# A latent-expert stage: norms split and moved, the second weights awaited at their first use

## The chip, the core and the metric

The kernel runs on one core of a Trainium2 chip. The metric is the device time of one execution in microseconds. The core has five engines that run their own instruction streams and meet through semaphores: TensorE (PE, matrix products and transposes), VectorE (DVE), ScalarE (ACT), GpSimd (POOL) and SyncE (SP, which issues the transfers here). Each stream is in order: an instruction that waits holds up all behind it on that engine.

## The reference, cut to what matters

The program is four blocks of attention and feed-forward. The change lies in the third feed-forward, a mixture of eight experts and a shared one, over 2048 tokens of width 256:

```
h = x @ down_w + down_b                      # latent, width 128
logits = x @ router_w + router_b - COST_LAMBDA * cost
probs = softmax(logits);  topv, topi = top_k(probs, 2);  gate = softmax(topv)
for k in range(2):
    mask = one_hot(topi[..., k], E)
    for e, (w1, b1, w2, b2) in enumerate(expert_params):
        hm = h * mask[..., e:e + 1]
        acc = acc + (gelu(gelu(hm) @ w1 + b1) @ w2 + b2)
    out = out + acc * gate[..., k:k + 1]
out = out + 0.1 * (gelu(gelu(h) @ shared_w1 + shared_b1) @ shared_w2 + shared_b2)
out = out @ up_w + up_b + gelu(x) @ core_w + core_b
```

Here x is the layer-normalized stream, and the result is added to the stream. An expert that a token did not choose still adds the constant gelu(b1) @ w2 + b2, which the kernel computes once.

## The kernel before, in words

The stage is the function latent_experts. Tokens are taken in four blocks b of 512. The hidden layers of all experts, laid side by side, are 21 tiles n of 128 rows, so that the main loop runs over G = 21 b + n, 84 steps in all, on every engine.

**One step of the main loop.** TensorE multiplies the block's latent by the first weights of the tile (hidden, lines 2330 to 2332). Each fp32 factor is held as a rounded upper part and a rest, so one product is three matmuls of 512 columns. ScalarE applies the gelu in place in PSUM (line 2258). VectorE multiplies by the gate row of the expert into the tile prod (line 2168), a ring of six slots. ScalarE rounds it (upper, line 2232, for the step two back), GpSimd subtracts to get the rest (h_low, line 2045), and TensorE multiplies both by the second weights (project, lines 2345 to 2347) four steps behind hidden. So hidden(G) needs prod of step G-3, and project(G-4) needs h_low of step G-4.

**What is woven into the first 13 steps.** The norms of blocks 1 to 3 are one buffer deep. For each block VectorE takes statistics (line 91) and aggregates them (line 95), GpSimd raises them to the power -1/2 (lines 114 and 116), VectorE applies the norm into ln.xn (line 102), TensorE transposes it (turn, line 2290) and multiplies by the router (route, line 2299, 16 matmuls of 8 columns), ScalarE copies the transposes out of PSUM (keep_turned, line 2195), and VectorE takes the logits (keep_logits, line 2071). After the logits of block 3 come the second softmax and the choice of experts for blocks 1 to 3 (shift, choose, place, weigh).

**Ahead of the loop.** The same is done for block 0, and with it: the first weights w1 are split (ScalarE line 2244, VectorE line 2148), the second weights w2 are split (ScalarE line 2249, VectorE line 2153), twenty small matmuls on w2 make the constant of the unchosen experts (line 2375; ScalarE keeps it at line 2251), the gates are transposed (line 2320) and kept (line 2220), written to memory and read back broadcast into the tile gb (line 2028), and the latent is split (ScalarE lines 2209 and 2213, VectorE line 2125). The raw w1 lies in the second half of gb and the raw w2 in the ring prod, so prod can't be written before w2 is split and the small matmuls are done. In the trace both weight tiles are called f_w_high and f_w_low, and f_gb and f_prod stand for their raw copies.

The order is written by hand: no planner sets it. The whole of the front part and the step numbers at which pieces are woven in stand in the four engine programs below.

Of the kernel before, what the change touches and what calls it, by code (L numbers as in the profile page):

```python
# [87 lines left out]
def layer_norm_stats(dve, n, b, source):  # L88

    for t in range(n.tiles):  # L90
        dve.bn_stats(n.stats[:, t, :], source(t)).then_inc(n.stats_done, 1)  # L91
    dve.wait_ge(n.stats_done, n.tiles * (b + 1))
    dve.memset(n.held[:, 0:1], 0.0)
    for t in range(n.tiles):
        dve.bn_aggr(n.mv[:, t, :], n.stats[:, t, :]).then_inc(n.meanvar_done, 1)
# [1836 lines left out]
def latent_experts(nc, tag, X, cst, PS, gate_rows, t):  # L1932
# [9 lines left out]
    with ExitStack() as ctx:  # L1942
# [61 lines left out]
        with nc.Block() as block:  # L2004
# [26 lines left out]
            @block.gpsimd  # L2031
            def _(pool):
                pool.memset(ln.eps[:, :], EPS).then_inc(preset, 1)
                pool.memset(neg_half[:, :], -0.5).then_inc(preset, 1)
                pool.memset(zb[:, :, :], 0.0).then_inc(preset, 1)
                pool.memset(gates[:, :, :], 0.0).then_inc(preset, 1)
                pool.wait_ge(preset, 4)
                pool.memset(gates[:, :, NE:NX], SHARED_GATE).then_inc(preset, 1)
                for b in range(NB - 1):
                    layer_norm_pool(pool, ln, b, neg_half)  # L2040
                for G in range(FULL):
                    pool.wait_ge(h_high_done, G + 1)
                    if G >= 6:
                        pool.wait_ge(y_done, G - 5)
                    pool.tensor_tensor(h_low[:, G % 6, :], prod[:, G % 6, :], h_high[:, G % 6, :].bitcast(F32),  # L2045
                                       ALU.subtract).then_inc(h_low_done, 1)
                    if G == 2:
                        layer_norm_pool(pool, ln, 3, neg_half)

            @block.vector  # L2050
            def _(dve):
# [7 lines left out]
                def source(b):  # L2059
                    return lambda k: X[:, TB * b + k, :]  # L2060

                def norm(b):

                    layer_norm_stats(dve, ln, b, source(b))
                    if b:
                        dve.wait_ge(transposed, KC * b)
                    layer_norm_apply(dve, ln, b, source(b))
# [66 lines left out]
                def add_bias(b, k):  # L2134
                    dve.tensor_tensor(X[:, TB * b + k, :], X[:, TB * b + k, :], outb[:, 0, :], ALU.add).then_inc(biased, 1)

                norm(0)
                dve.wait_ge(loaded_front, 64)
                then(dve.tensor_tensor(rb[:, :], rb[:, :], cst[:, C_COST:C_COST + NE], ALU.subtract))
                dve.wait_ge(gb1_done, 1)  # L2140
                for e in range(NE):
                    f = first[e]
                    z = dve.tensor_copy(zb[:, f:f + EXPERT_TILES[e], e], gb1[:, f:f + EXPERT_TILES[e]])
                z.then_inc(zb_done, 1)
                keep_logits(0)
                shift(0, 0, TB)
                dve.wait_ge(w1_high_done, 1)
                dve.tensor_tensor(w1_low[:, :, :], w1_in, w1_high[:, :, :].bitcast(F32), ALU.subtract).then_inc(w1_low_done, 1)
                choose(0, 0, TB)
                place(0, 0, TB)  # L2150
                weigh(0, 0, TB)
                dve.wait_ge(w2_high_done, 1)
                dve.tensor_tensor(w2_low[:, :, :], w2_in, w2_high[:, :, :].bitcast(F32), ALU.subtract).then_inc(w2_low_done, 1)
                latent_low(0)
                dve.wait_ge(loaded_back, 80)
                then(dve.tensor_tensor(outb[:, 0, :], outb[:, 0, :], outb[:, 1, :], ALU.add))
                norm(1)
                norm(2)
                dve.wait_ge(d_done, 1)
                for G in range(FULL):  # L2160
                    b, n = G // NHT, G % NHT
                    e = expert_of[n]
                    dve.wait_ge(act_done, G + 1)
                    if n == first[e]:
                        dve.wait_ge(gb_loaded[b % 2][e], 16 * (b // 2 + 1))
                    if G >= 6:
                        dve.wait_ge(h_low_done, G - 5)
                    dve.tensor_tensor(prod[:, G % 6, :], PS[:, HB[G % 3], :], gb[:, b % 2, e, :], ALU.mult).then_inc(prod_done, 1)  # L2168
                    if b == 0 and n in (4, 6, 9):
                        keep_logits((4, 6, 9).index(n) + 1)  # L2170
                    if b == 0 and n == 4:
                        norm(3)
                    if b == 0 and n == 9:
                        shift(1, TB, NT)
                    if b == 0 and n == 10:
                        choose(1, TB, NT)
                    if b == 0 and n == 11:
                        place(1, TB, NT)
                    if b == 0 and n == 12:
                        weigh(1, TB, NT)  # L2180
                    if n == 14 and b + 1 < NB:
                        latent_low(b + 1)
                    if n in (15, 16, 17, 18):
                        add_bias(b, n - 15)
                    if b and n in (9, 10):
                        add_outputs(b - 1, n - 9)
# [4 lines left out]
            def _(act):  # L2191
# [53 lines left out]
                exponent(0, 0, TB)  # L2245
                second(0, 0, TB)
                latent(0)
                act.wait_ge(loaded_w2, 16)
                act.activation(w2_high[:, :, :], w2_in, ACT.Copy).then_inc(w2_high_done, 1)
                act.wait_ge(d_done, 1)  # L2250
                act.activation(dsum[:, :], PS[0:NE, 3, 0:LAT], ACT.Copy).then_inc(d_kept, 1)
                keep_gates(0)
                act.wait_ge(c_done, 1)
                act.activation(consts[:, :], PS[0:NX, 3, LAT:2 * LAT], ACT.Copy).then_inc(c_kept, 1)
                for G in range(FULL):
                    b, n = G // NHT, G % NHT
                    act.wait_ge(h_done, G + 1)
                    act.activation(PS[:, HB[G % 3], :], PS[:, HB[G % 3], :], ACT.Gelu, bias=b1[:, n:n + 1]).then_inc(act_done, 1)  # L2258
                    if b == 0 and n in (2, 4, 7):
                        keep_turned((2, 4, 7).index(n) + 1)  # L2260
                    if G >= 2:
                        upper(G - 2)
                    if b == 0 and n == 10:
                        exponent(1, TB, NT)
                    if b == 0 and n == 11:
                        second(1, TB, NT)
                    if n == 4 and b:
                        keep_outputs(b - 1)
                    if n == 13 and b + 1 < NB:
                        latent(b + 1)  # L2270
                    if n in (17, 18):
                        core_input(b, n - 17)
                    if n == 15 and b + 1 < NB:
                        keep_gates(b + 1)
# [5 lines left out]
            def _(pe):  # L2280
# [53 lines left out]
                def project(G):  # L2334
                    b, n = G // NHT, G % NHT
                    out = PS[:, 2 + b % 2, :]
                    if n == 0:
                        pe.wait_ge(gT_kept, b + 1)
                        if b == 0:
                            pe.wait_ge(c_kept, 1)  # L2340
                        if b >= 2:
                            pe.wait_ge(y_kept, b - 1)
                        pe.matmul(out, consts[:, :], gT[0:NX, :], start=True, stop=False).then_inc(const_done, 1)
                    pe.wait_ge(h_low_done, G + 1)
                    pe.matmul(out, w2_high[:, n, :], h_high[:, G % 6, :], start=False, stop=False)
                    pe.matmul(out, w2_low[:, n, :], h_high[:, G % 6, :], start=False, stop=False)
                    pe.matmul(out, w2_high[:, n, :], h_low[:, G % 6, :], start=False, stop=(n == NHT - 1)).then_inc(y_done, 1)
# [33 lines left out]
                pe.matmul(PS[0:NX, 3, LAT:2 * LAT], cst[0:NX, C_BSUM:C_BSUM + NX], b2[:, :], start=False,  # L2381
                          stop=True).then_inc(c_done, 1)
                pe.wait_ge(w1_low_done, 1)
                pe.wait_ge(w2_low_done, 1)
                for G in range(FULL + LAG):
                    b, n = G // NHT, G % NHT
                    if G < FULL:
                        hidden(G)
                    if G >= LAG:
                        project(G - LAG)  # L2390
                    if G < FULL:
                        if b == 0 and n in (2, 4, 7):
                            turn((2, 4, 7).index(n) + 1)
                        if b == 0 and n in (3, 5, 8):
                            route((3, 5, 8).index(n) + 1)
                        if n == 12 and b + 1 < NB:
                            latent(b + 1)
                        if n == 14 and b + 1 < NB:
                            turn_gates(b + 1)
                        if b and n in (6, 8):  # L2400
                            outputs(b - 1, (n - 6) // 2)
# [603 lines left out]
```

## Time and profile before

| | us |
|---|---|
| median of 3 runs | 1897.74 |
| lowest and highest | 1887.23, 1900.02 |
| the profiled execution | 1893.01 |
| its span, first to last instruction | 1891.2 |

The page of the profile gives, over the whole span, TensorE 86% busy, VectorE 62%, ScalarE 46%, GpSimd 25%, at a mean granted TensorE clock of 0.939 of 2.4 GHz. The latent-expert stage is the stretch from about 1217 to 1434 us of it. Times in the rows are microseconds from the start of the span. A busy time of a matmul overlaps that of its neighbour, so the pace of TensorE is read from the distance between starts.

### The profile page before, as it was taken

The page shows a single profiled execution, that of the slowest core. Times are in us where ns is not written, and L with a number is a line of the kernel's source. Part 1 is how long each engine was busy: PE and PEld are TensorE (multiplying, and loading weights), DVE is VectorE, ACT ScalarE, POOL GpSimd, SP SyncE. Part 2 cuts the span into 40 slices and gives each one's busy share as a digit, 9 for nine tenths or more (in the row PEclk, how much of TensorE's full clock was granted, in tenths as well). Part 3 has the DMA queues.
Part 4 walks back from the last instruction along what each step waited for, and adds up shares of the span by engine and source line. Part 5 has one row for each costly group of instructions (what it writes and reads, how often), then busy time and mean ns, then how long its engine had stood idle before and what let it go on. Part 6 is the DMA issues. An engine that isn't in the chain of part 4 may idle for free. (4 is left out here: it accounts for less than half of the span.)

```text
span 1891.2 us, 28840 instructions
## 1 busy us (share of the span) xinstructions
PE 1619.8 (86%) x10648; PEld 945.2 (50%) x10654; DVE 1172.8 (62%) x2595; ACT 869.0 (46%) x1360; POOL 477.5 (25%) x594
## 2 busy tenths in 40 slices
PE   4899999899999999801599999779999999998776
PEld 2344444488756566501346655456775344443533
DVE  2687887333246666479767776355553787774475
ACT  1255666432225554541125555447672466665322
POOL 4222210033213330030323230026673422210100
PEclk9899999999999999955799999979999999999698
DMA  7342240100055424010345523111114345320322
GB/s 245 98 123 80 78 123 1 67 0 0 32 156 157 116 77 123 1 51 0 96 119 140 156 79 80 73 55 52 51 51 134 93 111 156 88 69 2 119 90 90
DMA packets 68688, 162.29 MB, mean 86 GB/s; under 512 B 10013, under 2 KB 15526, under 8 KB 67562
## 3 DMA queue, kind: packets, MB, share of 16 engines
q1 hardware_dynamic: 68554, 160.52, 29.9%
q8 instruction: 82, 1.34, 0.3%
q14 instruction: 52, 0.43, 0.1%
HBM read 111.06 MB, written 53.09 MB: 87 GB/s over the span
## 5 line engine op out<-in xcount | busy, mean ns | idle before, releaser
L1078 DVE TENSOR_REDUCE a_mx<-PS 128x1 f32<-128x512 f32 (+3 forms) x768 | 394.8, 552 | 191.6 <-PE PS L1320 129.1
L1261 ACT ACTIVATE a_pT<-PS 128x1024 f32<-128x1024 f32 (+3 forms) x384 | 310.4, 812 | 213.6 <-PE PS L1344 151.7
L1315 PE MATMUL PS<-a_k,a_q 64*128 64x512 f32 (+3 forms) x768 | 231.5, 413 | 10.5 <-DVE a_mx L1078 6.3
L405 DVE CUSTOM_DVE_ANT_0 PS<-PS,a_dist 128x448 f32<-128x448 f32 x256 | 156.2, 643 | 51.6 <-PE PS L650 49.3
L1335 PE MATMUL PS<-a_q,a_k 64*128 64x512 f32 (+3 forms) x768 | 172.0, 434 | 6.8 <-issue 5.0
L1358 PE MATMUL PS<-a_pT,a_va 128*32 128x512 f32 (+3 forms) x1536 | 163.6, 498 | 5.6 <-ACT a_raw L1219 5.4
L122 PE MATMUL PS<-cst 128*128 128x512 f32 x248 | 128.4, 646 | 44.2 <-PEq L66 35.3
L555 ACT ACTIVATE a_pT<-PS 128x448 f32<-128x448 f32 (+1 forms) x256 | 124.6, 540 | 86.3 <-PE PS L673 86.0
L1315 PEld LDWEIGHTS PS<-a_k,a_q 64*128 64x128 f32 x768 | 109.9, 185 | 79.2 <-DVE a_mx L1078 60.7
L1335 PEld LDWEIGHTS PS<-a_q,a_k 64*128 64x128 f32 x768 | 74.6, 183 | 143.4 <-issue 67.0
L2045 POOL TENSOR_TENSOR f_h_low<-f_prod,f_h_high 128x512 fp32r<-128x512 f32 x84 | 110.3, 1321 | 61.0 <-ACT f_h_high L2232 56.3
L2168 DVE TENSOR_TENSOR f_prod<-PS,f_gb 128x512 f32<-128x512 f32 x84 | 57.5, 688 | 70.2 <-ACT PS L2258 68.1
L650 PE MATMUL PS<-a_k,a_q 64*128 64x448 f32 x256 | 86.3, 465 | 12.7 <-DVE a_mx L405 5.5
L1196 ACT ACTIVATE a_q<-PS 16x1024 fp32r<-16x1024 f32 x48 | 48.8, 1016 | 91.8 <-PE PS L1366 91.4
L122 PEld LDWEIGHTS PS<-cst 128*128 128x128 f32 x248 | 45.0, 200 | 89.9 <-issue 81.8
L1318 PE MATMUL PS<-a_half_masks 64*128 64x128 bf16 x512 | 86.1, 227 | 0.0
L2258 ACT ACTIVATE PS<-PS,f_b 128x512 f32<-128x512 f32 x84 | 55.5, 660 | 50.6 <-PE PS L2332 50.3
L1320 PE MATMUL PS<-a_half_masks 64*128 64x64 bf16 x512 | 72.3, 189 | 0.0
L1029 POOL TENSOR_TENSOR a_mxh<-a_mx,a_m 128x16 fp32r<-128x16 f32 x48 | 10.9, 227 | 240.6 <-DVE a_mx L1078 240.6
L686 PE MATMUL PS<-a_pT,a_va 128*32 128x512 f32 x512 | 68.2, 604 | 1.5 <-ACT a_raw L563 1.1
L1506 POOL TENSOR_TENSOR f_h_low<-f_hid,f_h_high 128x512 fp32r<-128x512 f32 x32 | 41.1, 1289 | 101.9 <-ACT f_h_high L1571 101.9
L1083 DVE TENSOR_SCALAR a_q<-PS 16x1024 fp32r<-16x1024 f32 x48 | 59.0, 1230 | 6.0 <-PE PS L1366 4.6
(355 smaller groups left out, 3419.6 us busy)
## 6 DMA issues: line engine op xcount, KB each, us to landing
spread_scratch<-a_high SPq DMA_DIRECT2D x96, 256.0 KB, 3.5
a_q<-spread_scratch SPq DMA_DIRECT2D x96, 256.0 KB, 5.5
a_k<-spread_scratch SPq DMA_DIRECT2D x96, 256.0 KB, 6.5
f_gb<-gate_rows SPq DMA_DIRECT2D x68, 256.0 KB, 5.4
spread_scratch<-a_low SPq DMA_DIRECT2D x48, 256.0 KB, 4.5
a_q<-window_scratch SPq DMA_DIRECT2D x32, 256.0 KB, 5.4
a_k<-window_scratch SPq DMA_DIRECT2D x32, 256.0 KB, 6.3
window_scratch<-a_high SPq DMA_DIRECT2D x24, 256.0 KB, 4.7
```

Of the source, the lines that this page charges most:

```text
L122: pe.matmul(PS[:, bank, :], cst[:, C_ID:C_ID + P], cst[:, 0:512], start=True, stop=True)
L405: dve.tensor_tensor_reduce(PS[:, 4 + a, 0:KW], PS[:, 4 + a, 0:KW], dt_[:, off:off + KW], 1.0, 3e38, ALU.add, ALU.min, mx[:, gg % 2, qt, 2 ...
L555: act.activation(pT[rows, buffer_of(kt), 2 * half + a, GLOB:S], PS[rows, 2 * half + a, GLOB:S], ACT.Exp, scale=-float(slopes[2 * pair + a] ...
L650: pe.matmul(PS[:, 4 + a, 0:KW], q[rows, b % 2, pair, qt * P:(qt + 1) * P], k[rows, b % 2, pair, GLOB:S], start=True, stop=True).then_inc(s ...
L1078: dve.tensor_reduce(mx[:, gg % 2, qt, 2 * half + a:2 * half + a + 1], PS[:, 4 + a, 0:kw], AX.X, ALU.max).then_inc(max_done, 1)
L1261: act.activation(pT[:, N // 2 % 2, N % 2, :, q0:S], PS[:, 2 * (N % 2):2 * (N % 2) + 2, q0:S], ACT.Exp, scale=SCALE).then_inc(exp_done, 1)
L1315: mm = pe.matmul(ps[:, 0:kw], q[rows, b % 2, pair, qt * P:(qt + 1) * P], k[rows, b % 2, pair, 0:kw], start=True, stop=not causal)
L1318: pe.matmul(ps[:, kw - P:kw], half_masks[rows, 0, 0, :], half_masks[rows, 1, 0, :], start=False, stop=False)
L1320: mm = pe.matmul(ps[:, kw - 64:kw], half_masks[rows, 0, 1, :], half_masks[rows, 1, 1, 64:P], start=False, stop=True)
L1335: mm = pe.matmul(PS[:, 2 * half + a, q0:S], k[rows, b % 2, pair, kt * P:(kt + 1) * P], q[rows, b % 2, pair, q0:S], start=True, stop=not ca ...
L1358: mm = pe.matmul(PS[BLK * i:BLK * i + BLK, 6, q0:S], va[:, b % 2, kt, GH * g + i, :], pT[:, J % 2, i // 2, i % 2, q0:S], start=(kt == 0), ...
L2045: pool.tensor_tensor(h_low[:, G % 6, :], prod[:, G % 6, :], h_high[:, G % 6, :].bitcast(F32), ALU.subtract).then_inc(h_low_done, 1)
```

## The change

All of it is in latent_experts. The norm of a block is split into statistics and application, which can now stand apart. VectorE does both for block 1 before it reads the first logits, the statistics of block 2 before it splits w2, and applies block 2 after step 1 of the loop; block 3 has its statistics after step 3 and its application after step 5 (before: blocks 1 and 2 whole ahead of the loop, block 3 after step 4). The split of w1 on VectorE goes behind the softmax and the gates of block 0. ScalarE splits w2 behind the two copies that it stood ahead of. TensorE waits for the split w2 in project(0) and no longer ahead of the loop. The turns go from steps 2, 4, 7 to 0, 3, 6, the routes from 3, 5, 8 to 1, 4, 7. The sum of two bias rows moves from ahead of the loop to step 6.

```
@@ GpSimd
-                    if G == 2:
+                    if G == 1:
                         layer_norm_pool(pool, ln, 3, neg_half)
@@ VectorE
-                norm(0)
+                layer_norm_stats(dve, ln, 0, source(0))
+                normal(0)
...
+                layer_norm_stats(dve, ln, 1, source(1))
+                normal(1)
                 keep_logits(0)
                 shift(0, 0, TB)
-                dve.wait_ge(w1_high_done, 1)
-                dve.tensor_tensor(w1_low[:, :, :], w1_in, w1_high[:, :, :].bitcast(F32), ALU.subtract).then_inc(w1_low_done, 1)
                 choose(0, 0, TB)
                 place(0, 0, TB)
                 weigh(0, 0, TB)
+                dve.wait_ge(w1_high_done, 1)
+                dve.tensor_tensor(w1_low[:, :, :], w1_in, w1_high[:, :, :].bitcast(F32), ALU.subtract).then_inc(w1_low_done, 1)
+                latent_low(0)
+                layer_norm_stats(dve, ln, 2, source(2))
                 dve.wait_ge(w2_high_done, 1)
                 dve.tensor_tensor(w2_low[:, :, :], w2_in, w2_high[:, :, :].bitcast(F32), ALU.subtract).then_inc(w2_low_done, 1)
-                latent_low(0)
-                dve.wait_ge(loaded_back, 80)
-                then(dve.tensor_tensor(outb[:, 0, :], outb[:, 0, :], outb[:, 1, :], ALU.add))
-                norm(1)
-                norm(2)
                 dve.wait_ge(d_done, 1)
+                dve.wait_ge(w2_low_done, 1)
                 for G in range(FULL):
...
-                    if b == 0 and n in (4, 6, 9):
-                        keep_logits((4, 6, 9).index(n) + 1)
-                    if b == 0 and n == 4:
-                        norm(3)
+                    if b == 0 and n in (2, 5, 8):
+                        keep_logits((2, 5, 8).index(n) + 1)
+                    if b == 0 and n == 1:
+                        normal(2)
+                    if b == 0 and n == 3:
+                        layer_norm_stats(dve, ln, 3, source(3))
+                    if b == 0 and n == 5:
+                        normal(3)
+                    if b == 0 and n == 6:
+                        dve.wait_ge(loaded_back, 80)
+                        then(dve.tensor_tensor(outb[:, 0, :], outb[:, 0, :], outb[:, 1, :], ALU.add))
@@ ScalarE
                 latent(0)
-                act.wait_ge(loaded_w2, 16)
-                act.activation(w2_high[:, :, :], w2_in, ACT.Copy).then_inc(w2_high_done, 1)
                 act.wait_ge(d_done, 1)
                 act.activation(dsum[:, :], PS[0:NE, 3, 0:LAT], ACT.Copy).then_inc(d_kept, 1)
                 keep_gates(0)
+                act.wait_ge(loaded_w2, 16)
+                act.activation(w2_high[:, :, :], w2_in, ACT.Copy).then_inc(w2_high_done, 1)
...
-                    if b == 0 and n in (2, 4, 7):
-                        keep_turned((2, 4, 7).index(n) + 1)
+                    if b == 0 and n in (0, 3, 6):
+                        keep_turned((0, 3, 6).index(n) + 1)
@@ TensorE
                         if b == 0:
                             pe.wait_ge(c_kept, 1)
+                            pe.wait_ge(w2_low_done, 1)
...
                 pe.wait_ge(w1_low_done, 1)
-                pe.wait_ge(w2_low_done, 1)
...
-                        if b == 0 and n in (2, 4, 7):
-                            turn((2, 4, 7).index(n) + 1)
-                        if b == 0 and n in (3, 5, 8):
-                            route((3, 5, 8).index(n) + 1)
+                        if b == 0 and n in (0, 3, 6):
+                            turn((0, 3, 6).index(n) + 1)
+                        if b == 0 and n in (1, 4, 7):
+                            route((1, 4, 7).index(n) + 1)
```

VectorE between the gates of block 0 and the first products of the loop. Before (f_w_low<-f_prod is the split of w2, the L91 to L102 rows are norms):

```order
L2118 TENSOR_TENSOR f_gates<-f_hots 128x4x8
L2153 TENSOR_TENSOR f_w_low<-f_prod,f_w_high 128x2688
L2125 TENSOR_TENSOR f_lat_low<-f_lat,f_lat_high 128x512
L2156 TENSOR_TENSOR f_outb<-f_outb 128x256
L91 BN_STATS f_ln_stats<-X 128x6 x4
```

and now (f_w_low<-f_gb is the split of w1):

```order
L2117 TENSOR_TENSOR f_gates<-f_hots 128x4x8
L2153 TENSOR_TENSOR f_w_low<-f_gb,f_w_high 128x2688
L2124 TENSOR_TENSOR f_lat_low<-f_lat,f_lat_high 128x512
L91 BN_STATS f_ln_stats<-X 128x6 x4
L93 MEMSET f_ln_held 128x1
L95 BN_AGGR f_ln_meanvar<-f_ln_stats 128x2 x4
L2157 TENSOR_TENSOR f_w_low<-f_prod,f_w_high 128x2688
L2168 TENSOR_TENSOR f_prod<-PS,f_gb 128x512 x2
L102 TENSOR_SCALAR f_ln_xn<-X,f_ln_meanvar,f_ln_rstd 128x256 x4
```

The two whole norms that stood between the split latent and the first product are gone from there; one half norm and the split of w2 stand there instead, and the application of block 2 stands behind two products.

TensorE at the start of the loop. Before:

```order
L2381 MATMUL PS<-f_b,cst 9x128
L2330 MATMUL PS<-f_lat_high,f_w_high 128x512
L2331 MATMUL PS<-f_lat_low,f_w_high 128x512
L2332 MATMUL PS<-f_lat_high,f_w_low 128x512
L2330 MATMUL PS<-f_lat_high,f_w_high 128x512
L2331 MATMUL PS<-f_lat_low,f_w_high 128x512
L2332 MATMUL PS<-f_lat_high,f_w_low 128x512
```

and now:

```order
L2389 MATMUL PS<-f_b,cst 9x128
L2337 MATMUL PS<-f_lat_high,f_w_high 128x512
L2338 MATMUL PS<-f_lat_low,f_w_high 128x512
L2339 MATMUL PS<-f_lat_high,f_w_low 128x512
L2297 MATMUL PS<-cst,f_ln_xn 128x128 x8
L2337 MATMUL PS<-f_lat_high,f_w_high 128x512
L2338 MATMUL PS<-f_lat_low,f_w_high 128x512
L2339 MATMUL PS<-f_lat_high,f_w_low 128x512
L2306 MATMUL PS<-f_router,f_xnT 128x8 x8
```

The turn of block 1 now stands after one step instead of three, and its route after two instead of four.

## Rows read from the trace of the kernel before

**Rows 1.** Stretches of the stage: start:end, length, busy time by engine (instructions), PEclk, DMA.

```profile
1240.00:1255.00 15.00, 7.17 (x22) 4.75 (x22) 10.78 (x31) 5.23 (x10) 2.41 (x4) 0.51 0.50 160
...
1255.00:1272.00 17.00, 17.00 (x65) 13.33 (x66) 5.81 (x16) 6.36 (x11) 6.25 (x6) 0.63 0.00 0
...
1285.00:1300.00 15.00, 11.12 (x36) 7.74 (x35) 11.78 (x43) 11.19 (x18) 7.04 (x6) 0.77 0.02 4
...
1320.00:1420.00 100.00, 99.44 (x409) 73.27 (x407) 51.90 (x75) 72.23 (x124) 71.45 (x54) 1.00 0.15 48
```

**Rows 2.** The same view in slices of 2 us; PEclk is the granted clock.

```profile
1240.00:1242.00 2.00, 0.67 (x4) 0.37 (x4) 0.84 (x1) 1.76 (x3) 0.00 (x0) 0.58 0.00 0
...
1266.00:1268.00 2.00, 2.00 (x8) 1.70 (x8) 0.00 (x0) 1.66 (x4) 0.14 (x1) 0.60 0.00 0
```

**Rows 3.** TensorE in order of time: start, duration, work [idle before <-releaser].

```profile
1232.96 4.53 PE L2375 MATMUL PS<-f_prod,f_zb 128*8 128x128 f32 x40
...
1238.27 0.63 PE L2320 MATMUL PS<-cst,f_gates 128*128 128x128 f32 x4 [0.78 <-DVE f_gates L2118]
...
1244.86 0.76 PE L2330 MATMUL PS<-f_lat_high,f_w_high 128*128 128x512 f32 x1 [2.51 <-DVE f_lat_low L2125]
1245.42 0.63 PE L2331 MATMUL PS<-f_lat_low,f_w_high 128*128 128x512 f32 x1
1245.85 0.63 PE L2332 MATMUL PS<-f_lat_high,f_w_low 128*128 128x512 f32 x1
...
1255.00 0.80 PE L2330 MATMUL PS<-f_lat_high,f_w_high 128*128 128x512 f32 x1 [3.21 <-DVE f_prod L2168]
...
1261.27 2.07 PE L2343 MATMUL PS<-f_gT,f_consts 9*128 9x512 f32 x2
...
1270.38 0.39 PE L2331 MATMUL PS<-f_lat_low,f_w_high 128*128 128x512 f32 x1
1270.61 0.39 PE L2332 MATMUL PS<-f_lat_high,f_w_low 128*128 128x512 f32 x1
...
1273.80 1.10 PE L2290 MATMUL PS<-cst,f_ln_xn 128*128 128x128 f32 x8 [0.70 <-DVE f_ln_xn L102]
...
1276.13 1.85 PE L2299 MATMUL PS<-f_router,f_xnT 128*128 128x8 f32 x16
1277.83 0.47 PE L2330 MATMUL PS<-f_lat_high,f_w_high 128*128 128x512 f32 x1
```

**Rows 4.** VectorE in order of time, same columns.

```profile
1234.67 0.18 DVE L2085 TENSOR_REDUCE f_den<-f_probs 128x4 f32<-128x32 f32 x1
...
1237.96 0.19 DVE L2118 TENSOR_TENSOR f_gates<-f_hots 128x32 f32<-128x32 f32 x1
1241.16 2.96 DVE L2153 TENSOR_TENSOR f_w_low<-f_prod,f_w_high 128x2688 fp32r<-128x2688 f32 x1 [3.01 <-ACT f_w_high L2249]
...
1245.09 1.40 DVE L91 BATCH_NORM_STATS2 f_ln_stats<-X 128x6 f32<-128x256 f32 x4
...
1248.38 1.38 DVE L102 TENSOR_SCALAR f_ln_xn<-X,f_ln_meanvar,f_ln_rstd 128x256 f32<-128x256 f32 x4 [1.47 <-POOL f_ln_rstd L116]
...
1254.26 1.88 DVE L2168 TENSOR_TENSOR f_prod<-PS,f_gb 128x512 f32<-128x512 f32 x3
...
1270.49 3.26 DVE L102 TENSOR_SCALAR f_ln_xn<-X,f_ln_meanvar,f_ln_rstd 128x256 f32<-128x256 f32 x4 [5.90 <-POOL f_ln_rstd L116]
```

**Rows 5.** ScalarE in order of time, same columns.

```profile
1232.85 0.23 ACT L2199 ACTIVATE f_probs<-f_expo 128x32 f32<-128x32 f32 x1
...
1238.70 2.43 ACT L2249 ACTIVATE f_w_high<-f_prod 128x2688 fp32r<-128x2688 f32 x1
...
1251.82 0.60 ACT L2195 ACTIVATE f_xnT<-PS 128x512 f32<-128x512 f32 x1 [0.26 <-PE PS L2290]
```

**Rows 6.** GpSimd in order of time, same columns.

```profile
1270.35 1.29 POOL L2045 TENSOR_TENSOR f_h_low<-f_prod,f_h_high 128x512 fp32r<-128x512 f32 x1
```

**Rows 7.** Transfers into the tile gb, 1240 to 1300 us: issue to landing.

```profile
DMA to landing us min/median/max: 3.1/4.4/7.0
```

More of the change, by code:

```diff
@@ L2060, in source, with normal @@
                     return lambda k: X[:, TB * b + k, :]
-                def norm(b):
-                    layer_norm_stats(dve, ln, b, source(b))
+                def normal(b):
                     if b:
```

## The prediction, made before the changed kernel was run

> **What bounds the kernel now.** I read the stretches of the stage first. From 1320 to 1420 us TensorE is busy 99.44 of 100 us at the full clock [rows 1]: the main loop is bound by TensorE, and nothing in it is touched beyond step 12. The time to be had lies at its start. From 1240 to 1255 TensorE is busy 7.17 of 15 us at a granted 0.51, and from 1255 to 1272 it is busy throughout, but at a mean of 0.63 [rows 1]. The 2 us slices place the two ends of this: the clock fell from 2.4 to 1.2 GHz within 1240 to 1242 (0.58) and rose again within 1266 to 1268 (0.60) [rows 2]. What TensorE did before it fell: its small matmuls on w2 ended at 1237.49 (1232.96 + 4.53), the gate transposes at 1238.90, and then it mostly waited; the first step of the loop starts at 1244.86, released by the rest of the latent on VectorE [rows 3]. It waits once more, 3.21 us to 1255.00, for the first products of VectorE [rows 3], which start only at 1254.26 [rows 4], behind two whole norms.
>
> What clock it has is seen in the pace of equal matmuls: 0.43 us from start to start at 1245 (1245.42 to 1245.85), 0.23 at 1270 (1270.38 to 1270.61) [rows 3].
>
> As the finish line I take the start of hidden(9), now at 1277.83 [rows 3]. By then both orders have issued the same work on TensorE: 9 steps of hidden, 5 of project, three turns and three routes. Behind it the order is as before, apart from the last logits, one step earlier, and TensorE sets the pace to the end of the stage, so what is won there should reach the end.
>
> **Ahead of the loop.** The exponentials of block 0 were ready at 1233.08 (1232.85 + 0.23) [rows 5], but their sum started at 1234.67, since the split of w1 stood between [rows 4]. With that split behind the gates, the sum starts 1.6 us earlier and the gates are done at 1236.55 in place of 1238.15 (1237.96 + 0.19) [rows 4]. Then comes the split of w1, as large as that of w2, 2.96 us [rows 4], to 1239.5, and the rest of the latent. Before, hidden(0) started 0.74 us after the split in front of it ended (1241.16 + 2.96 = 1244.12, to 1244.86) [rows 3, 4]; so now at 1240.3. That is **4.6 us earlier**. The 3.01 us that VectorE waited for ScalarE's half of w2 [rows 4] go: that half, 2.43 us [rows 5], now stands behind the gate copy. The gates can be transposed when the small matmuls end, 1237.5, so they are copied by about 1238.8, w2's upper part is ready at 1241.2, and the first gelu is not held up by more than some tenths.
>
> The norm of block 1 costs nothing: VectorE has no work between its first rows of the stage and the logits of block 0, while TensorE warms up, turns and routes. If that cover were gone, it would cost a norm, some 3.2 us (1.82 for statistics and aggregation, from 1245.09 to 1246.91, where the wait before 1248.38 begins, and 1.38 to apply) [rows 4].
>
> VectorE goes on after the latent at 1240.25: statistics of block 2, 1.82, to 1242.1, split of w2, 2.96, to 1245.0, first product. It was at 1254.26 [rows 4], **9.3 us earlier**. This product also needs the first gate row from memory. The gates are kept at 1238.8; if store and load both took the shortest landing of this tile, 3.1 us, the row would be there at 1245.0, if both took the median, 4.4, at 1247.6 [rows 7]. The store is far smaller than one load (9 rows against 128), so I take the lower value and no wait; the upper end, less what step 2 covers, is 2 us.
>
> **The loop to hidden(9), at the full clock.** Work: 9 x 3 + 5 x 3 = 42 matmuls at 0.233 are 9.8 us; three turns of 1.10, 3.3; three routes of 1.70 (1276.13 to 1277.83), 5.1; the product of constants at half of its 2.07 at the low clock, 1.0 [rows 3]. Sum 19.2. Waits, following each stream:
> - route(1) waits for the copies of turn(1). First gelu to 1242.1, two copies of 0.60 [rows 5] to 1243.3; TensorE is there at 1242.8: 0.5.
> - turn(2) waits for the norm of block 2. Products 0 and 1 take VectorE to 1246.3, the four applications 1.38 [rows 4] to 1247.6; TensorE is there at 1246.4: 1.2.
> - turn(3) waits for the norm of block 3, behind gelu(5) and product 5: 1256.5 against 1255.6: 0.9.
>
> Together 2.6. On GpSimd the powers of block 3 now stand ahead of h_low(2), and wait for statistics that VectorE takes only after product 3, about 1250.8. h_low(2) then ends near 1253.4 and project(2) wants it at 1254.9: 1.5 us of slack, so I cost it at nothing; were it late, project and ScalarE's ring behind it would be late by the same.
>
> One more price: at 1270.49 the four applications took 3.26 us in place of 1.38, while GpSimd ran the h_low of 1270.35, 1.29 long, right behind its power [rows 4, 6]. Both applications now fall beside an h_low (of steps 0 and 3). Bounds 0 and 1.9 each; there is one h_low in the way and no power, so I take 1.2 each, **2.4**. The Trainium skill, page SBUF — State Buffer, section Who interferes with whom, speaks against the change here: VectorE and GpSimd share a port pair under an exclusive lock, a tensor_scalar in a 2-port mode takes it, and the later one is fully blocked for the whole instruction of the other. By that rule each application batch would lose what is left of one h_low, at most 1.29, and the gain would be 13.1; by the row alone, 3.8 for both, 11.9.
>
> So hidden(9) starts at 1240.3 + 19.2 + 2.6 + 2.4 = 1264.5, **13.3 us earlier**. Before, the same work took 33.0 us (1244.86 to 1277.83), now 24.2. The bias sum at step 6 and its wait are short and the transfer has long landed; nothing.
>
> **The baseline.** The sum is against one execution of 1893.0 us, 4.7 under the median of three that span 12.8. I take the middle of the two, 1895.4, as what a median is likely to show: 1895.4 - 13.3 = **1882**. One per cent, about what a measurement of this kernel tells from no change, is 19 us: faster than 1879.
>
> **Rivals.**
> - *The clock falls all the same, and rises on the way.* Between 1237.5 and 1240.3 TensorE has only gate transposes and two products of 8 and 9 rows, then turns and routes between the steps. For it: it fell at 1240 after just such work [rows 2, 3]. Against it: it fell with TensorE mostly idle after 1238.90, and now the gap there is under 1 us and later ones at most 2.4. If it falls and rises at hidden(4), which at 0.43 a matmul starts 3.6 us later than at 0.23, the gain is 9; if it rises only after turn(3), some 9.5 are lost and 4 stay. Middle 7: 1888. Chance 0.22.
> - *The second cold stretch goes too.* From 1285 to 1300 the mean was 0.77 [rows 1], that is 2 x 0.23 x 15 = 6.9 us at 1.2 GHz; at 0.233 in place of 0.43 they shrink by 3.2. For it: little, the softmax and its waits of steps 9 to 13 are unchanged; but whether a gap drops the clock may turn on chance. Gain 16.5: 1879. Chance 0.12.
> - *Slower.* The clock falls at 1240 and does not rise before step 12, since from step 0 on every third step carries a turn or a route, and before it stayed low for 12 us of unbroken work of this mix (1255 to 1267) [rows 1, 2]. Work to hidden(9) is then twice 19.2, with the waits covered: 1278.7, 0.9 later than before. Six steps of hidden and project more, 36 matmuls at 0.19 extra, add 7.0, less the 3.9 that TensorE idles in 1285 to 1300 [rows 1]: 4 us slower in all, 1899. It decides only if no rise comes before step 9. Against it: the rise at 1267 came in the midst of a turn and steps. Chance 0.05.
> - *The first rows of gb land late, or the applications pay in full*: the gain is 10 to 11. This lies in the range of the main case.
>
> The main case has 0.56; 0.05 is left for what I do not see. Its own range is 1876 to 1889, from the spread of the runs and the bounds above. The whole range, with most of the first two rivals, is 1873 to 1893. Faster by over 1%: most of what lies under 1879, from the second rival and the lower part of the main case, 0.20. Slower by over 1% needs 1917, which no case gives: 0.03. Within 1%: 0.77.
>
> **What would show it.** Hidden(0) some 2.8 us after the gate transposes begin, in place of 6.6; first product 4.7 us after it, in place of 9.4; turn(1) right behind hidden(0). Granted clock near 1.0 through steps 0 to 8, matmuls at 0.23 apart. From hidden(0) to hidden(9) 24 us in place of 33.0. Four applications of over 2 us beside an h_low. Waits of about 1 us of the turns for ln_xn, and no wait of project for h_low before step 9. From hidden(9) to the end of the stage as long as before. The forecast is wrong if the clock in steps 0 to 8 is well below 1, if the first product waits for gb, or if what is won at hidden(9) is missing at the end of the stage.

## The result, and the profile after

Over eleven runs each, the changed kernel takes 1882.46 us in the median (1870.55 to 1886.30), the kernel before 1893.29 (1887.09 to 1900.02). The ratio on record is 0.9921, with a 95% interval of 0.9901 to 0.9940: faster by 15.0 us (11.4 to 18.7), less than the 1% that I had set as a clear change. The listed times alone give less: the medians lie 10.8 us apart, the means 13.1. Why the ratio comes out larger than both isn't known from the record, so the gain of the whole kernel is 11, 13 or 15 us by the figure that one takes. The profiled execution took 1886.3 us, its span was 1884.5.

The two profiled spans differ by only 6.7 us, and this misleads: the stage began at 1227.75 after the change and at 1217.39 before, 10.4 us later for reasons that lie ahead of it. So all that follows counts from the start of the stage, its first table load on ScalarE (the loading of a function table before an activation). Its three parts (to the start of hidden(0), from there to hidden(9), from there to the first norm of the next stage), in the columns of [rows 1], in the changed kernel:

```profile
1227.75:1250.65 22.90, 16.71 (x84) 10.16 (x85) 14.24 (x66) 11.60 (x14) 4.54 (x9) 0.85 0.43 157
1250.65:1273.47 22.82, 21.15 (x116) 17.21 (x117) 15.41 (x38) 12.95 (x23) 12.61 (x10) 0.93 0.31 105
1273.47:1429.84 156.37, 146.74 (x589) 106.76 (x588) 80.55 (x156) 107.67 (x181) 103.02 (x80) 0.99 0.14 46
```

and before:

```profile
1217.39:1244.86 27.47, 17.09 (x84) 10.14 (x85) 14.04 (x54) 12.47 (x15) 3.33 (x7) 0.79 0.37 135
1244.86:1277.83 32.97, 28.28 (x117) 22.02 (x117) 17.22 (x51) 13.17 (x22) 11.59 (x13) 0.65 0.22 69
1277.83:1434.69 156.86, 148.27 (x591) 107.67 (x590) 80.46 (x155) 107.07 (x179) 102.31 (x80) 0.98 0.14 46
```

4.57 us came from the first part, 10.15 from the second, 0.5 from the third: the stage went from 217.3 to 202.1 us, by 15.2, which is what the ratio says and more than the medians show. In the second part the mean granted clock rose from 0.65 to 0.93. TensorE at its joints:

```profile
1250.65 0.56 PE L2337 MATMUL PS<-f_lat_high,f_w_high 128*128 128x512 f32 x1 [1.61 <-DVE f_lat_low L2124]
...
1257.97 1.10 PE L2297 MATMUL PS<-cst,f_ln_xn 128*128 128x128 f32 x8
...
1267.96 1.09 PE L2297 MATMUL PS<-cst,f_ln_xn 128*128 128x128 f32 x8 [1.67 <-DVE f_ln_xn L102]
```

The first answers to the step that started at 1244.86 in [rows 3]. The wait of 3.21 us ahead of hidden(3) is gone, and so is a shorter one ahead of turn(1), which before was

```profile
1249.82 1.97 PE L2290 MATMUL PS<-cst,f_ln_xn 128*128 128x128 f32 x8 [0.78 <-DVE f_ln_xn L102]
```

Turn(3) waits longer than before, 1.67 us in place of 0.70. The clock did fall, 0.2 us after hidden(0) had started, but was back 3.4 us later (both worked out from the slices below, where 1.00 is 2.4 GHz and 0.50 is 1.2 GHz). Before, the same fall lasted 27 us, between the two slices in [rows 2]:

```profile
1250.00:1252.00 2.00, 1.35 (x4) 0.99 (x5) 1.96 (x8) 1.63 (x2) 0.00 (x0) 0.72 0.12 39
1252.00:1254.00 2.00, 2.00 (x10) 1.91 (x9) 2.00 (x5) 1.44 (x3) 1.68 (x1) 0.50 0.88 300
1254.00:1256.00 2.00, 2.00 (x17) 1.87 (x15) 1.85 (x3) 1.07 (x2) 1.92 (x2) 0.92 0.83 242
```

VectorE, the rows that answer to [rows 4], and one of GpSimd:

```profile
1252.16 2.92 DVE L2157 TENSOR_TENSOR f_w_low<-f_prod,f_w_high 128x2688 fp32r<-128x2688 f32 x1
1255.17 1.45 DVE L2168 TENSOR_TENSOR f_prod<-PS,f_gb 128x512 f32<-128x512 f32 x2
1256.53 1.38 DVE L102 TENSOR_SCALAR f_ln_xn<-X,f_ln_meanvar,f_ln_rstd 128x256 f32<-128x256 f32 x4
...
1265.62 2.28 DVE L102 TENSOR_SCALAR f_ln_xn<-X,f_ln_meanvar,f_ln_rstd 128x256 f32<-128x256 f32 x4
```

```profile
1252.32 2.82 POOL L114 TENSOR_TENSOR f_ln_vareps<-f_ln_meanvar,f_ln_eps 128x4 f32<-128x4 f32 x1 [15.84 <-DVE f_ln_meanvar L95]
```

The first product starts 27.42 us into the stage, before 36.87. The tiny addition on GpSimd, 0.20 us elsewhere, took 2.82, ending with the split of w2 on VectorE that it met. It cost nothing here: the power behind it was done at 1256.23, before VectorE came to the applications at 1256.53.

### The profile page after: what moved, and what is told of

It is laid out like the page before. It is cut to its first block and busy times, and to the rows that moved or that the text cites. A ratio compares the mean times of both kernels' runs of the same rounds, so it can differ in the third digit from the quotient of the medians.

```text
span 1884.5 us, 28841 instructions
## 1 busy us (share of the span) xinstructions
PE 1621.0 (86%) x10648; PEld 942.4 (50%) x10654; DVE 1172.1 (62%) x2595; ACT 868.4 (46%) x1360; POOL 481.1 (26%) x594
## 5 line engine op out<-in xcount | busy, mean ns | idle before, releaser
L1315 PE MATMUL PS<-a_k,a_q 64*128 64x512 f32 (+3 forms) x768 | 232.0, 414 | 10.4 <-DVE a_mx L1078 6.3
L2265 ACT ACTIVATE PS<-PS,f_b 128x512 f32<-128x512 f32 x84 | 55.5, 660 | 44.1 <-PE PS L2339 43.9
L665 PE MATMUL PS<-a_q,a_k 64*128 64x448 f32 (+1 forms) x256 | 60.8, 465 | 2.4 <-DVE a_q L411 2.4
```

The source lines that it names most:

```text
L1315: mm = pe.matmul(ps[:, 0:kw], q[rows, b % 2, pair, qt * P:(qt + 1) * P], k[rows, b % 2, pair, 0:kw], start=True, stop=not causal)
```

## The experiments

Parts in us, and the whole stage; "rest" is the span less the stage. Each is one profiled execution. "Warm" means that idle time of TensorE is filled: keep_busy(pe, PS, cst, bank, count) issues that many dummy products of 512 columns into a bank that is not in use, and nothing reads them. The edits are cut to what they change.

| kernel | to hidden(0) | to hidden(9) | to the end | stage | rest |
|---|---|---|---|---|---|
| before | 27.47 | 32.97 | 156.86 | 217.3 | 1673.9 |
| before again, e9 | 27.64 | 32.98 | 157.89 | 218.5 | 1670.4 |
| changed | 22.90 | 22.82 | 156.37 | 202.1 | 1682.4 |
| changed again, e10 | 22.97 | 22.67 | 156.90 | 202.5 | 1671.5 |
| e1 front only | 22.96 | 36.41 | 156.94 | 216.3 | 1672.1 |
| e2 norms only | 27.76 | 26.75 | 156.88 | 211.4 | 1675.8 |
| e3 w2 ahead | 27.37 | 28.27 | 156.61 | 212.3 | 1675.8 |
| e4 before, warm | 27.59 | 28.60 | 156.01 | 212.2 | 1678.4 |
| e5 w2 ahead, warm | 27.38 | 21.75 | 155.13 | 204.3 | 1671.7 |
| e6 changed, warm | 22.99 | 25.09 | 156.97 | 205.1 | 1674.9 |
| e7 block 3 earlier | 22.82 | 21.30 | 156.65 | 200.8 | 1676.7 |
| e8 exponentials paired | 22.78 | 22.70 | 158.54 | 204.0 | 1675.6 |
| e11 dummies first | 18.93 | 24.49 | 157.52 | 200.9 | 1681.4 |
| e12 together | 19.49 | 19.56 | 157.67 | 196.7 | 1671.2 |

**Repeats, e9 and e10.** No edit.

> The kernel before, unchanged, profiled a second time, to see how much the length of the stage moves between executions. Theory (the stage before is long in every execution, since its idle stretches are set by its order): hidden(0) 27.5, first product 36.9, hidden(9) 58 to 61, stage 215 to 219. Rival (a good part of the 15.2 us is the luck of when the clock falls and rises): stage under 212.

> The changed kernel, unchanged, profiled a second time. Theory: hidden(0) 22.9, first product 27.4, stage 200 to 205, where the clock may fall at one place or another (2 to 3 us each). Rival (the first profile was a lucky one): stage over 207.

Both met the theory: the stages repeated to within 1.2 and 0.5 us, down to where the clock fell. The rest moved between 1670 and 1682 us, whatever the kernel, so most of the spread of the runs seems to come from there. The rivals, luck in one profile or the other, would need a stage about 5 us away from its first value, and are out. A difference of about 1 us between two stages is no more than one kernel shows with itself.

**e1**, the front part alone: the kernel before with the two splits moved on VectorE (below), the split of w2 moved on ScalarE, and TensorE's wait for w2 put into project(0).

```
 choose; place; weigh
+w1_low; latent_low(0)
 w2_low
-latent_low(0)
 outb; norm(1); norm(2)
```

> The kernel before with only the part of the change that lies ahead of the loop: the split of w1 behind the gates on VectorE, the split of w2 behind the two copies on ScalarE, and TensorE's wait for w2 in project(0). The norms, turns and routes stand as before. Times are counted from the start of the stage (first table load of ScalarE in it); before: hidden(0) 27.5, first product 36.9, hidden(9) 60.4, stage 217.3; changed: 22.9, 27.4, 45.7, 202.1. Theory (the loop is set by when VectorE gets to the first product, and by the clock that follows): hidden(0) at 22.9, but the first product at 36.4, since both whole norms still stand before it; TensorE is starved in between, so hidden(9) at 59 to 61 and a stage of 216 to 218. Rival (the earlier start of the loop is what pays): hidden(9) 4.6 earlier, 55.8, stage 212.7.

The theory held: hidden(9) at 59.4, the stage 216.3. TensorE after hidden(2):

```profile
1250.42 1.97 PE L2291 MATMUL PS<-cst,f_ln_xn 128*128 128x128 f32 x8 [5.04 <-DVE f_ln_xn L102]
...
1255.61 0.80 PE L2331 MATMUL PS<-f_lat_high,f_w_high 128*128 128x512 f32 x1 [3.22 <-DVE f_prod L2169]
```

Hidden(0) came 4.5 us earlier, and TensorE then waited for the same norms. Of the 15.2 us this half wins 1.0, which is no more than the stage before moved by itself. The clock fell just behind hidden(0) and came back after 3.4 us, as in the changed kernel; then it fell again in the wait of 5.04 us.

**e2**, the norms, turns and routes alone. On VectorE as below; ScalarE's order and TensorE's wait for w2 are those of the kernel before as well.

```
-choose; place; weigh; w1_low; latent_low(0); stats(2); w2_low
+w1_low; choose; place; weigh; w2_low; latent_low(0); stats(2)
```

> The changed kernel with the two splits, ScalarE's order and the wait for w2 put back as before: only the norms, turns and routes are moved. Times from the start of the stage as above. Theory: hidden(0) back at 27.5, first product at 29.4 (it needs hidden(0) and its gelu), 2 us later than in the changed kernel; hidden(9) 2 to 5 later, 48 to 51, stage 204 to 207, so that this part holds 10 to 13 of the 15.2 us. Rival (the clock decides: TensorE idles 5 us ahead of hidden(0) and the clock then stays at 1.2 GHz through turns and routes up to turn(3)): hidden(9) at 55 or later, stage 211 or more.

The theory failed, and the rival came out nearly as written: the stage was 211.4 (it said 211 or more) and hidden(9) came at 54.5 (it said 55). The first product came at 30.3, 0.9 later than the theory had it, but the clock, which fell in the idle time ahead of hidden(0), came back only 12.3 us after hidden(0), in the middle of step 4:

```profile
1250.73 0.77 PE L2337 MATMUL PS<-f_lat_high,f_w_high 128*128 128x512 f32 x1 [2.51 <-DVE f_lat_low L2124]
...
1262.66 0.64 PE L2337 MATMUL PS<-f_lat_high,f_w_high 128*128 128x512 f32 x1
1263.14 0.39 PE L2338 MATMUL PS<-f_lat_low,f_w_high 128*128 128x512 f32 x1
```

Alone the two halves win 1.0 and 5.9 us, together 15.2. Each takes away one of two gaps, and only without both do the wait and the long stretch at the low clock go.

**e3**, the wait for w2 put back.

```
                 pe.wait_ge(w1_low_done, 1)
+                pe.wait_ge(w2_low_done, 1)
```

> The changed kernel with TensorE's wait for the split w2 put ahead of the loop again, nothing else. Times from the start of the stage as above. Theory: hidden(0) when the split of w2 ends, at 27.3 in place of 22.9, first product behind its gelu at 29.4 in place of 27.4, hidden(9) 2 to 4 later, 47.7 to 50, stage 204 to 206. Rival (the wait is free, since the first product waits for the same split in any case): hidden(9) within 1 of 45.7, stage 202 to 203.

Both expectations failed: this one line costs 10.2 us (stage 212.3, hidden(9) at 55.6).

```profile
1241.07 0.38 PE L2389 MATMUL PS<-f_b,cst 9*9 9x128 f32 x2
1247.59 0.76 PE L2337 MATMUL PS<-f_lat_high,f_w_high 128*128 128x512 f32 x1 [6.14 <-DVE f_w_low L2157]
```

```profile
1247.59:1275.86 28.27, 28.27 (x116) 23.36 (x117) 11.14 (x28) 12.26 (x21) 9.73 (x9) 0.66 0.15 49
```

From hidden(0) to hidden(9) TensorE never waits, and still needs 28.3 us, at a clock of 0.66. The clock had fallen in the idle time and came back 12.6 us after hidden(0). Then it fell once more, for 6.8 us, with TensorE at work without a break:

```profile
1258.22:1260.22 2.00, 2.00 (x10) 1.90 (x9) 1.51 (x6) 1.55 (x3) 1.25 (x1) 0.50 0.00 0
1260.22:1262.22 2.00, 2.00 (x7) 0.82 (x6) 1.67 (x9) 1.90 (x4) 1.12 (x1) 0.99 0.00 0
1262.22:1264.22 2.00, 2.00 (x16) 1.91 (x15) 0.07 (x1) 0.00 (x0) 1.92 (x4) 0.86 0.00 0
1264.22:1266.22 2.00, 2.00 (x7) 1.79 (x8) 0.00 (x0) 0.00 (x0) 0.63 (x1) 0.50 0.00 0
```

So a wait isn't the only thing that a fall can follow; what stood there was a route, 16 matmuls of 8 columns. e5 asks what of the 10.2 us is the clock.

**e5**, e3 with the idle time filled.

```
+                keep_busy(pe, PS, cst, 2, 7)
                 pe.wait_ge(w1_low_done, 1)
                 pe.wait_ge(w2_low_done, 1)
```

> The kernel of e3 (wait for w2 ahead of the loop) with its 6.1 us of idle TensorE before hidden(0) filled by seven dummy products, 5.6 us at the full clock. Times from the start of the stage; e3: hidden(0) 27.4, hidden(9) 55.6, stage 212.3; changed: 22.9, 45.7, 202.1. Theory (most of what the early wait costs is the clock that falls in its idle time): clock at 1.0 through the loop, hidden(0) still at 27.4 or 27.6, hidden(9) at 49 to 50.5, stage 205.5 to 207: the wait itself costs 4 to 5, the clock 5 to 6. Rival (the order does it, the clock is by the way): hidden(9) at 54 or later.

```profile
1239.52 6.28 PE L122 MATMUL PS<-cst 128*128 128x512 f32 x14
1245.23 0.80 PE L2337 MATMUL PS<-f_lat_high,f_w_high 128*128 128x512 f32 x1
```

```profile
1245.23:1266.98 21.75, 19.90 (x118) 15.97 (x117) 11.02 (x28) 11.68 (x21) 8.78 (x8) 1.00 0.19 70
```

The stage fell by 8.0 us to 204.3 with hidden(0) where it was, 6.5 of it before hidden(9) and 1.5 behind it. Hidden(9) at 49.1 met the theory, the stage came out below it. Filling the idle time gives back 8.0 of e3's 10.2 us. The other 2.2 are not the price of the wait, though, since e5 and the changed kernel differ in clock as well: in e5 it stayed at 2.4 GHz to the end of the stage, while in the changed kernel it was low for 3.4 us before hidden(9) and for 3.4 behind it. Part by part e5 loses 4.5 us ahead of hidden(0) and wins back 1.1 and 1.2 in the two others. At equal clocks the wait would cost some 4.5 to 5 us; that is an estimate from these differences, no run shows it.

**e4**, the kernel before with its idle time filled.

```
+                keep_busy(pe, PS, cst, 2, 3)
                 pe.wait_ge(d_kept, 1)
...
+                keep_busy(pe, PS, cst, 2, 3)
                 pe.wait_ge(w1_low_done, 1)
...
+                    if G == 3:
+                        keep_busy(pe, PS, cst, 2, 4)
```

> The kernel before with idle TensorE filled: six dummy products (3 before the wait for dsum, 3 before hidden(0)) and four before hidden(3), on a bank that is not yet in use; it computes the same. This takes the low clock away and leaves the order. Times from the start of the stage as above. Theory: clock at 1.0 from the small matmuls on, hidden(0) at 27.5, first product at 36.9 and hidden(3) at 37.6 as before, then the work to hidden(9) at full clock, 16 us and a wait of about 1: hidden(9) at 54.6, stage 211.5; so the clock is some 6 of the 15.2 us and the order the rest. Rival (the clock is nearly all of it): hidden(9) under 50. Rival (dummy products hold TensorE up or do not keep the clock): hidden(9) at 59 or later.

5.1 us, near the theory's 6, though the clock fell twice more before hidden(9), to a mean of 0.88 there. TensorE still waited 2.62 us for the norm of block 1, and hidden(3), behind its four dummies, started 0.6 us later in the stage than before. The order before has waits that no clock removes.

**e6**, the changed kernel with its gap filled.

```
+                keep_busy(pe, PS, cst, 2, 2)
                 pe.wait_ge(w1_low_done, 1)
```

> The changed kernel with its 1.6 us of idle TensorE before hidden(0) filled by two dummy products. In the profiled run of the changed kernel the clock was at 1.2 GHz for 3.4 us from just before hidden(0). Theory: the clock stays at 2.4 GHz, hidden(0) as before at 22.9 to 23.1, hidden(9) 1 to 1.7 earlier, at 44.0 to 44.7, stage 200.5 to 201. Rival (the waits of the turns take it up, or the dummies delay hidden(0)): hidden(9) at 45.5 or later, stage 202 or more.

The rival. The clock held past hidden(0), and the stage was 2.5 to 3 us longer than in the two profiles of the changed kernel. VectorE, GpSimd and TensorE show why:

```profile
1248.19 0.69 DVE L2168 TENSOR_TENSOR f_prod<-PS,f_gb 128x512 f32<-128x512 f32 x1 [0.56 <-DMA f_gb<-gate_rows]
1248.80 2.32 DVE L102 TENSOR_SCALAR f_ln_xn<-X,f_ln_meanvar,f_ln_rstd 128x256 f32<-128x256 f32 x4
```

```profile
1249.24 1.40 POOL L2045 TENSOR_TENSOR f_h_low<-f_prod,f_h_high 128x512 fp32r<-128x512 f32 x1 [1.25 <-ACT f_h_high L2239]
```

```profile
1251.18 1.09 PE L2297 MATMUL PS<-cst,f_ln_xn 128*128 128x128 f32 x8 [2.52 <-DVE f_ln_xn L102]
```

Product 1 now waited for its gate row, the norm behind it slid beside the first h_low and took 2.32 us, turn(2) waited 2.52, and the clock fell after all, just ahead of hidden(5), for 3.4 us.

**e7**, the norm of block 3 applied one step earlier.

```
-                    if b == 0 and n == 5:
+                    if b == 0 and n == 4:
                         normal(3)
```

> The changed kernel with the application of block 3's norm after step 4 instead of 5. In the changed kernel turn(3) waited 1.67 us for it, and it took 2.28 us beside an h_low, while VectorE had idled 2.83 us just before product 5. Theory: turn(3) does not wait, hidden(9) 1.5 earlier, at 44.2, stage 200.5. Rival (GpSimd's h_low of step 2 holds the four applications up, over 3 us, and delays product 5 and the ring behind it): gain under 0.5, stage 201.6 or more.

The theory held: turn(3) did not wait, turn(2) waited 0.32 us, hidden(9) came at 44.1, and 1.3 to 1.8 us of the stage were won.

**e8**, the two exponentials of the second softmax side by side.

```
                         exponent(1, TB, NT)
+                        second(1, TB, NT)
-                    if b == 0 and n == 11:
-                        second(1, TB, NT)
```

> The changed kernel with the two exponentials of the second softmax side by side on ScalarE after step 10, so that two table loads of 1.28 us go, and ScalarE waits for VectorE's difference in between (some 2 us). Theory (table loads on ScalarE make project wait 0.70, 2.36 and 1.07 us in steps 11 to 14): these 4.1 us shrink to about 2, and the second stretch at 1.2 GHz (1.7 us of clock loss) may go as well: from hidden(9) to the end 154.5 in place of 156.4. Rival (the wait for the difference takes the place of the loads): 156 to 157.

Worse than the rival had it: two table loads went, but ScalarE waited 2.04 us for the difference, project 2.95 for h_low, and the last part grew from 156.4 to 158.5 us, where the rival said 157 at most. The clock fell twice there in place of once.

**e11**, the dummies and the first turn ahead of the wait for loads.

```
-                pe.wait_ge(loaded_front, 64)
                 keep_busy(pe, PS, cst, 0, 4)
                 turn(0)
+                pe.wait_ge(loaded_front, 64)
```

> The changed kernel with TensorE's wait for the first four loads moved behind the four dummy products and the first turn, which need none of them. In the changed kernel TensorE idled 5.9 us at the start of the stage, the clock fell, and the dummies then ran 6.5 us at 1.2 GHz while the norm of block 0 had been ready for 5.3 us. Theory (this start is on the path to hidden(0)): turn(0) at 5 to 6 in place of 10.2, hidden(0) 3.5 to 4.5 earlier at 18.4 to 19.4, stage 198. Rival (the loads of w1 and w2 then bind: w2 was issued at 2.3 and such a load took 8.7 to land): hidden(0) at 20.5 or later, stage 200 or more.

```profile
1222.01 3.67 PE L122 MATMUL PS<-cst 128*128 128x512 f32 x8 [2.10 <-PEq L66]
1226.91 1.09 PE L2297 MATMUL PS<-cst,f_ln_xn 128*128 128x128 f32 x8 [1.23 <-DVE f_ln_xn L102]
...
1249.63 1.09 PE L2297 MATMUL PS<-cst,f_ln_xn 128*128 128x128 f32 x8 [2.23 <-DVE f_ln_xn L102]
```

The dummies ran at the full clock and hidden(0) came 4.0 us earlier, as the theory had it, but only 1.1 to 1.6 stayed, in place of 4: product 1 waited 0.53 us for its gate row and turn(2) 2.23 us, by the same chain as in e6, and the last part was 0.6 to 1.2 us longer, with the clock low for 6.8 us of it in place of 3.4.

**e12**, e7 and e11 together, with block 2's statistics moved behind the shift and its application behind product 0.

```
                 shift(0, 0, TB)
+                layer_norm_stats(dve, ln, 2, source(2))
...
-                    if b == 0 and n == 1:
+                    if b == 0 and n == 0:
                         normal(2)
```

> What the runs pointed to, together: the dummy products and the first turn ahead of the wait for loads (e11), block 3 applied after step 4 (e7), and block 2's norm pulled apart further: its statistics behind the shift of block 0, where VectorE waits 1.2 us for the exponentials, and its application after product 0 in place of product 1. In e11 and e6 product 1 waited 0.5 us for a gate row, the application then took 2.3 us beside the first h_low, and turn(2) waited 2.2 to 2.5 us. Theory (the order around products 0 and 1 is what gave back half of e11's earlier start): hidden(0) at 19.5, turn(2) waits under 0.7, hidden(9) at 41, stage 197 to 199; against the kernel before a ratio of 0.989 to 0.991. Rival (what is gained at the start goes into the clock, which falls elsewhere): stage 200 to 202, ratio 0.992 as the changed kernel.

```profile
1237.42:1256.98 19.56, 19.38 (x117) 15.92 (x118) 13.77 (x29) 12.61 (x23) 8.93 (x8) 1.00 0.35 121
```

The second part is down to 19.56 us at the full clock, 19.38 of it busy, and turn(2) doesn't wait. The last part took 157.7 us, about 1 more than in the changed kernel, with the clock low for 6.8 us of it in place of 3.4, so some of the gain went there. The stage is 5.4 to 5.8 us shorter than in the changed kernel. Timed, it is 1877.07 us in six runs, a ratio of 0.9909 (0.9879 to 0.9940) against the kernel before. By the interval this is not yet told apart from the changed kernel's 0.9921; that it is better rests on the length of the stage.

## Why the prediction was right

The mechanism was right: the time lay ahead of hidden(9), in a late first step, a late first product and a low clock, and the change moved all three. That 1882 us was forecast and 1882.46 measured is closer than the parts deserve. The baseline was taken as 1895.4, from one execution and a median of three, and came out as 1893.29, 2.1 us lower. The gain was put at 13.3; it is 10.8 by the medians, 15.0 by the ratio and 15.2 by the stage. By the medians the two errors, 2.1 and 2.5, nearly cancel, and that is luck. Step by step:

- **Ahead of the loop:** 4.6 us forecast, 4.57 measured; first product 9.3, measured 9.45. e1 shows that alone this is worth 1 us.
- **The waits before:** I wrote that TensorE waits "once more", 3.21 us. Between hidden(0) and hidden(9) it also waited 0.78 and 0.70 for norms, 4.7 us in all.
- **Work to hidden(9):** 19.2 us forecast. e12, nearly free of waits and cold stretches, needed 19.56.
- **Waits and port:** this term was mis-sized. Forecast were waits of 0.5, 1.2 and 0.9 us, 2.6 in all, and 2.4 for the two batches of applications beside an h_low. Measured were 0, 0 and 1.67, and the 1.67 holds the whole price of the port, 0.9 (2.28 us for the four applications of block 3 in place of 1.38). Block 2's applications met no h_low (1.38): hidden(2), and with it the first h_low, came late, which I put down to the low clock. e6 and e11 bear that out: as soon as the clock held, those applications took 2.3 us in place of 1.4.
- **The clock:** the sum has the full clock throughout, and the mean was 0.93. My first rival gave a fall at 1240 a chance of 0.22 and a loss of 3.6 to 9.5 us (for a rise at hidden(4) the gain left would be 13.3 - 3.6 = 9.7, where I wrote 9). The clock fell, for 3.4 us, and cost about 1.7 (an estimate: half of them, since all fell on matmuls). With 19.2 and 1.67 that makes 22.6 of the 22.82 measured, where 24.2 was forecast. So the second part came out near by two errors against each other, which is luck too: 5.0 us of waits where 1.7 were, no time at the low clock where 3.4 us were. How cheap the fall was could not be read from the trace of before; e2 and e3 show it at its dear end, back only 12.3 and 12.6 us after hidden(0), though TensorE was unbroken at work.
- **Gate rows:** costed at nothing, upper end 2 us. Right for the changed kernel; in e6 and e11 product 1 waited 0.5 us for its row, and turn(2), behind it and the slowed applications, waited over 2.
- **Slower:** half of the rival's mechanism is seen in e3, a low clock that outlasts 12.6 us of unbroken work and comes back for 3.4 us only. Even there the stage was 5 us shorter than before; no kernel here had a longer stage than the one before.
- **Past hidden(9):** as forecast, the gain reached the end; the last part was 0.5 us shorter. The second rival, that the later stretch at the low clock goes too, came half true: it was 3.4 us long in place of 6.8. In e9, where it was 6.8 again, the last part was 1 us longer than in the first profile of before, so 0.5 says little.

What stays open is why the clock is back 3.4 us after its fall in one case and 17 in others. The short case went with 1.6 us idle ahead of hidden(0) (changed kernel, e1), the long one with 2.5 us, after 2.4 more a little earlier, and with 6.1 us (e2, e3), and the runs show no more than that. Nor do they show why it fell in e3, e4 and e6 in the midst of work. That e5's gain is the clock alone is inferred from equal starts of hidden(0).

## What to carry to other kernels

Count idle TensorE twice where the clock falls in it: once as the wait, and once as the slow work behind it. In e3, filling the idle time with dummy products, which removes only the second, gave back 8.0 of 10.2 us. But measure it: the same remedy made the changed kernel 2.5 to 3 us slower (e6), since the steps that came earlier ran into a gate row and GpSimd. Two gaps in a row are one problem: the halves of this change alone won 1.0 and 5.9 us, both together 15.2. And when a stretch is made tighter, look for what is next in line by tenths of a microsecond, here a gate row and a GpSimd instruction, since it decides whether the next gain is kept.

## What the runs showed of the hardware

The same 42 matmuls, turns and routes took 19.6 us at 2.4 GHz and 28.3 at a mean of 0.66, both without a wait worth naming (e12, e3). With dummy matmuls in the idle time the clock stayed at 2.4 GHz (e5). It fell in idle time, but in e3 also with TensorE busy in the whole of the slices before it. Four VectorE applications of 128x256 beside one GpSimd h_low of 1.3 us took 2.3 us in place of 1.4 (changed kernel, e6, e11). A GpSimd addition of 128x4 that started 0.16 us after a VectorE subtraction of 128x2688 took 2.82 us in place of 0.20: here GpSimd was held up by VectorE, the direction that I had not priced. By the Trainium skill, SBUF — State Buffer, section Who interferes with whom, a VectorE instruction with two SBUF inputs contends with a GpSimd instruction that reads SBUF, and the trace agrees.
